# Ten small embedding tables loaded eight rows to a partition, one comparison in eight on ScalarE, and another order of units at both ends of a recommendation tower

## The reference

```
e = jnp.stack([tbl_0[ids[:, 0]], ..., tbl_25[ids[:, 25]]], axis=1)     # 2048 x 26 x 128
combined = jnp.concatenate([e, r_dense_x[:, None, :]], axis=1)
interact = jnp.einsum('bfd,bgd->bfg', combined, combined)
z = interact[:, triu_i, triu_j]                                        # 351 pairs
h = jnp.concatenate([z, r_dense_x], axis=1)
h = jnp.maximum(h @ W_top1 + b_top1, 0.0)                              # 479 -> 512
h = jnp.maximum(h @ W_top2 + b_top2, 0.0)                              # 512 -> 256
y = h @ W_top3
```

## Time and profile before

| what | value |
|---|---|
| median of 3 runs | 373.95 us (373.89 to 375.94) |
| the profiled execution | 373.27 us, of which the span is 371.4 us |
| mean granted TensorE clock | 0.986 |
| TensorE matmuls busy | 335.2 us (90%) |
| GpSimd busy | 257.3 us (69%) |
| VectorE busy | 238.5 us (64%) |
| ScalarE busy | 121.9 us (33%) |

### The profile page before, as it was taken

One profiled execution on the slowest core, in us unless ns is written; L12 is line 12 of the kernel. 1 busy time (PEld: TensorE's weight loads), 2 busy tenths in 40 slices (PEclk: granted clock), 3 DMA queues, 4 the chain that ended last, 5 costly groups with the idle time before them and its releaser, 6 DMA issues.

```text
span 371.4 us, 9558 instructions
## 1 busy us (share of the span) xinstructions
PE 335.2 (90%) x4024; PEld 310.7 (84%) x4024; DVE 238.5 (64%) x385; ACT 121.9 (33%) x229; POOL 257.3 (69%) x271
## 2 busy tenths in 40 slices
PE   0656879999999999999999999999999999967896
PEld 0646879788898999899889999899889989857795
DVE  6995499599485966679276957689277946010010
ACT  2473221332233323342233323242333224241422
POOL 5877787777777777777777777777777777775000
PEclk9998898999999999999999999999999999999999
DMA  7976228344244443434243433434243413334020
GB/s 188 287 202 196 77 73 259 91 114 101 58 120 102 123 98 98 121 104 113 58 121 100 126 91 107 112 109 113 59 136 89 117 51 108 83 108 116 19 69 4
DMA packets 40351, 41.02 MB, mean 110 GB/s; under 512 B 17119, under 2 KB 33983, under 8 KB 40308
## 3 DMA queue, kind: packets, MB, share of 16 engines
q1 hardware_dynamic: 30737, 22.44, 22.2%
q0 software_dynamic: 8448, 17.32, 17.4%
q10 hardware_dynamic: 1123, 0.64, 0.7%
HBM read 33.01 MB, written 7.36 MB: 109 GB/s over the span
## 4 chain that ended last, share of the span: by engine, by line
PE 79%; POOL 6%; DMA 4%; DVE 3%; issue 3%; ACT 3%; SPq 1%; ACTq 0%
PE ps_o L616 36%; PE ps_g L643 15%; PE ps_l L667 10%; PE ps_l L693 7%; PE ps_t L628 6%; POOL rows L257 6%; PE ps_l L669 3%; ACT h L404 2%; DMA turn<-gram 2%; DMA rows<-tbl,idx 2%; DVE onehot L525 1%; DVE tab L515 1%; PE ps_l L713 1%; DMA idx<-ids_g 1%; ACT emb L382 1%
## 5 line engine op out<-in xcount | busy, mean ns | idle before, releaser
L257 POOL DMA_INDIRECT rows<-tbl,idx x264 | 256.4, 971 | 82.9 <-issue 79.0
L525 DVE TENSOR_SCALAR onehot<-ids_b,row_of 128x513 fp32r<-128x513 int16 (+1 forms) x304 | 201.5, 740 | 18.3 <-PE ps_o L616 16.2
L616 PE MATMUL ps_o<-onehot,tab 128*128 128x256 f32 (+1 forms) x1216 | 163.4, 292 | 19.2 <-DVE tab L515 13.7
L616 PEld LDWEIGHTS ps_o<-onehot,tab 128*128 128x128 f32 (+1 forms) x1216 | 153.0, 194 | 24.7 <-issue 20.1
L539 DVE COPY gram<-ps_g 128x432 f32<-128x432 f32 x32 | 19.5, 608 | 93.1 <-PE ps_g L643 81.4
L375 ACT COPY emb<-ps_o 128x512 f32<-128x512 f32 x38 | 30.3, 797 | 129.1 <-PE ps_o L616 129.1
L643 PEld LDWEIGHTS ps_g<-emb 128*54 128x54 f32 x2048 | 54.7, 132 | 10.8 <-ACT emb L382 4.7
L643 PE MATMUL ps_g<-emb 128*54 128x54 f32 x2048 | 58.4, 216 | 5.2 <-ACT emb L382 3.5
L382 ACT COPY emb<-ps_t 128x512 f32<-128x512 f32 x66 | 43.0, 674 | 1.0 <-PE ps_t L628 0.7
L628 PE MATMUL ps_t<-ident,rows 128*128 128x128 f32 x264 | 39.0, 276 | 3.9 <-DMA rows<-tbl,idx 3.2
L667 PE MATMUL ps_l<-z,w_sb 117*128 117x256 f32 x168 | 40.9, 379 | 1.7 <-issue 1.7
(11 more groups left out here) (27 smaller groups left out, 50.0 us busy)
## 6 DMA issues: line engine op xcount, KB each, us to landing
turn<-gram SPq DMA_DIRECT2D x62, 91.1 KB
ids_b<-ids_oh SPq DMA_DIRECT2D x35, 129.0 KB, 3.6
rows<-tbl,idx POOLq DMA_INDIRECT x264
z<-turn SPq DMA_DIRECT2D x64, 40.5 KB
stage<-tbl SPq DMA_DIRECT2D x10, 256.0 KB, 5.3
stage<-tbl SPq DMA_DIRECT2D x10, 192.0 KB
turn<-gram SPq DMA_DIRECT2D x62, 21.1 KB
xs<-x SPq DMA_DIRECT2D x8, 128.0 KB, 2.2
```

The lines of the kernel that those rows point to most:

```text
L257: nc.gpsimd.indirect_dma_start(out=rows[m % RING][:, i, :], out_offset=None, in_=gathered[GATHERED.index(f)] if f in GATHERED else oh_tabl ...
L525: nc.vector.tensor_scalar(onehot[n % BUFS][0:r, 0:FILL].rearrange("p (a b) -> p a b", a=RUNS), ids_b[0:r, o, :, 0:RUN], row_of[0:r, h:h + ...
L616: last = nc.tensor.matmul(ps_o[n % 2][:, j, :], tab[0:r, UNIT * o + j, part, k, :], onehot[m % BUFS][0:r, STEP * j:STEP * (j + 1)], start= ...
```

## The change

A table is now one chunk: row 8p+k is in partition p, 125 partitions of 4 KB each, loaded by two DMAs (112 and 13 partitions), cast by one instruction and subtracted by one. The stages are 6 of 4 KB instead of 11 of 2 KB a partition. The comparison of fill h matches the rows 8p+h.

In steps 0 and 1 ScalarE makes the last fill of each unit (8 of them) in two instructions: the distance |index - row|, then max(0, 1 - distance). VectorE leaves these out.

At the start TensorE does unit (1,0) ahead of quad (0,4) and products(0), and every further unit of step 1 one place earlier. VectorE makes the comparisons of unit (1,0), the low parts of tables 6 and 7 and four comparisons more ahead of `keep_gram(0)`. In the loop TensorE does `unit(t + 1, 4)` ahead of `layer3(t - 1)`. At t = 6 it does `products(13)`, `unit(7, 4)`, `layer3(5)`, where it did `layer3(5)`, `unit(7, 4)`, `products(13)`; ScalarE and VectorE keep in that order. SyncE loads indices in another order at the start; its loop is as it was.

```diff
-KT = -(-OH_ROWS // P)
+KT = 8
+OH_P = OH_ROWS // KT
+ACT_STEPS = 2
+PIECES = ((0, OH_P // 16 * 16), (OH_P // 16 * 16, OH_P))
...
+def act_makes(t, h):
+    return t < ACT_STEPS and h == FILLS - 1
...
-        NSTAGE = 11
-        with nc.sbuf_tensor("stage", [P, NSTAGE, 512], F32) as stage:
+        NSTAGE = 6
+        with nc.sbuf_tensor("stage", [P, NSTAGE, KT * D], F32) as stage:
...
+        def made_by_act(t, o):
+            return min(unit_at(t, o) + 1, unit_at(ACT_STEPS, 0))
+        def made_by_dve(t, o, h):
+            return fill_at(t, o, h) + 1 - made_by_act(t, o) + (act_makes(t, FILLS - 1) and h < FILLS - 1)
...
             def load_ids(t, o):
                 if t and o < units_of(t - 1):
-                    sp.wait_ge(onehot_made, fill_at(t - 1, o, FILLS - 1) + 1)
+                    sp.wait_ge(onehot_made, made_by_dve(t - 1, o, FILLS - 1))
+                    if act_makes(t - 1, FILLS - 1):
+                        sp.wait_ge(onehot_act, made_by_act(t - 1, o))
...
+            def load_chunk(n):
+                if n >= NSTAGE:
+                    sp.wait_ge(chunk_l, n - NSTAGE + 1)
+                rows_of = oh_tables[n].rearrange("(p k) d -> p (k d)", k=KT)
+                for a, b in PIECES:
+                    sp.dma_start(stage[a:b, n % NSTAGE, :], rows_of[a:b, :]).then_inc(chunk_in[n % NSTAGE], 16)
...
-            for c in range(4, NCHUNKS):
-                load_chunk(c)
-                if c == NCHUNKS - 4:
-                    for o in range(UNITS):
+            for n in range(2, NOH):
+                load_chunk(n)
+                if n == NOH - 3:
+                    load_ids(1, 3)
+                    load_ids(1, 4)
+                    for o in range(FIRST_UNITS):
                         load_ids(1, o)
             load_x(1)
+            load_ids(2, 0)
             spread(0)
-            sp.wait_ge(chunk_l, NCHUNKS)
+            load_ids(2, 1)
+            load_ids(2, 2)
+            sp.wait_ge(chunk_l, NOH)
             fetch_z(0)
             load_weights()
-            for o in range(UNITS):
-                load_ids(2, o)
+            load_ids(2, 3)
+            load_ids(2, 4)
...
+            def make(t, o): 
+                n = fill_at(t, o, FILLS - 1)
+                act.wait_ge(ids_in[o], ids_loaded(t, o))
+                if n >= BUFS:
+                    act.wait_ge(onehot_used, n - BUFS + 1)
+                to = onehot[n % BUFS][0:OH_P, 0:FILL]
+                nc.scalar.activation(to.rearrange("p (a b) -> p a b", a=RUNS), ids_b[0:OH_P, o, :, 0:RUN], ACT.Abs, bias=last_row[0:OH_P]
+                                     ).then_inc(distance_made, 1)
+                act.wait_ge(distance_made, made_by_act(t, o))
+                nc.scalar.activation(to, f32(to), ACT.Relu, bias=1.0, scale=-1.0).then_inc(onehot_act, 1)
...
+            act.wait_ge(row_made, 2)
+            make(0, 0)
+            chunk(0)
+            chunk(1)
             keep_x(0)
+            chunk(2)
+            chunk(3)
+            make(0, 1)
             keep_unit(0, 0)
             keep_quad(0, 0)
+            chunk(4)
+            make(0, 2)
+            chunk(5)
             keep_unit(0, 1)
             keep_quad(0, 1)
+            chunk(6)
+            make(1, 0)
             keep_unit(0, 2)
             keep_quad(0, 2)
             keep_quad(0, 3)
+            chunk(7)
+            make(1, 1)
+            keep_unit(1, 0)
             keep_quad(0, 4)
             keep_gram(0)
...
@@ vector @@
-            makes(0, 0, FILLS)
+            makes(0, 0, 4)
+            chunk(0)
+            makes(0, 4, FILLS)
+            chunk(1)
+            for n in range(2, UNIT * FIRST_UNITS):
+                makes(0, FILLS // 2 * n, FILLS // 2 * (n + 1))
+                chunk(n)
             makes(1, 0, FILLS)
+            chunk(6)
+            chunk(7)
+            makes(1, FILLS, FILLS + 4)
             keep_gram(0)
+            makes(1, FILLS + 4, 3 * FILLS)
+            chunk(8)
+            chunk(9)
+            makes(1, 3 * FILLS, ALL)
             keep_gram(1)
             makes(2, 0, BUFS)
...
-                keep_y(t - 1)
-                keep_gram(b)
-                makes(t + 2, FILLS, BUFS)
+                if t < STEPS - 2:
+                    keep_y(t - 1)
+                    keep_gram(b)
+                    makes(t + 2, FILLS, BUFS)
+                else:
+                    keep_gram(b)
+                    keep_y(t - 1)
...
@@ tensor @@
             quad(0, 3)
+            unit(1, 0)
             quad(0, 4)
             products(0)
-            unit(1, 0)
+            unit(1, 1)
             quad(1, 0)
...
                 quad(b, 3)
-                layer3(t - 1)
-                unit(t + 1, 4)
-                products(b)
+                if t < STEPS - 2:
+                    unit(t + 1, 4)
+                    layer3(t - 1)
+                    products(b)
+                else:
+                    products(b)
+                    unit(t + 1, 4)
+                    layer3(t - 1)
```

More of the change, by code:

```diff
@@ L159, in tower_kernel, with chunk_count, parts_of @@
         f32 = lambda ap: ap.bitcast(F32)
[L162 to L189, removed]
+        def chunk_count(n):
+            return 16 * len(PIECES) * (n // NSTAGE + 1)
+        def parts_of(n):
+            return stage[0:OH_P, n % NSTAGE, :], [tab[0:OH_P, n, part].rearrange("p k d -> p (k d)") for part in range(2)]
         def unit_at(t, o):
@@ L364, in _, with chunk @@
         def _(act):
-            def chunk(c):
-                act.wait_ge(chunk_in[c % NSTAGE], chunk_count(c))
-                for _, at, hi, _ in chunk_parts(c):
-                    last = nc.scalar.copy(hi, at)
-                last.then_inc(chunk_h, 1)
+            def chunk(n):
+                act.wait_ge(chunk_in[n % NSTAGE], chunk_count(n))
+                at, (hi, _) = parts_of(n)
+                nc.scalar.copy(hi, at).then_inc(chunk_h, 1)
+            def make(t, o):
[8 more added lines that the diff above has]
+                nc.scalar.activation(to, f32(to), ACT.Relu, bias=1.0, scale=-1.0).then_inc(onehot_act, 1)
             def keep_unit(t, o):
@@ L606, in unit @@
                 if t < 2:
-                    pe.wait_ge(chunk_l, 2 * UNIT * (o + 1))
+                    pe.wait_ge(chunk_l, UNIT * (o + 1))
                 for h in range(FILLS):
                     m = fill_at(t, o, h)
-                    pe.wait_ge(onehot_made, m + 1)
-                    for i in range(KB):
-                        k = KB * h + i
-                        r = chunk_rows(k)
-                        for j in range(UNIT):
-                            for part in range(2):
-                                last = nc.tensor.matmul(
-                                    ps_o[n % 2][:, j, :], tab[0:r, UNIT * o + j, part, k, :],
-                                    onehot[m % BUFS][0:r, STEP * j:STEP * (j + 1)], start=(k, j, part) == (0, 0, 0),
-                                    stop=(k, j, part) == (KT - 1, UNIT - 1, 1), skip_group_check=True)
+                    if act_makes(t, h):
+                        pe.wait_ge(onehot_act, made_by_act(t, o))
+                    else:
+                        pe.wait_ge(onehot_made, made_by_dve(t, o, h))
+                    for j in range(UNIT):
+                        for part in range(2):
+                            last = nc.tensor.matmul(
+                                ps_o[n % 2][:, j, :], tab[0:OH_P, UNIT * o + j, part, h, :],
+                                onehot[m % BUFS][0:OH_P, STEP * j:STEP * (j + 1)], start=(h, j, part) == (0, 0, 0),
+                                stop=(h, j, part) == (KT - 1, UNIT - 1, 1), skip_group_check=True)
                     last.then_inc(onehot_used, 1)
```

90 lines of the change are left out of this document (36 added, 54 removed).

## The result

The changed kernel takes 364.5 us (median of 4 runs, 363.89 to 365.45), the kernel before, run beside it, 374.88: ratio 0.9725, 95% interval 0.9683 to 0.9767. It is faster, by more than I forecast (367.5, range 365.8 to 372.9). The profiled execution took 364.55 us with a span of 362.7, against 373.27 and 371.4: 8.7 us less in both.

The account below looks back on a forecast made before the run. TensorE's path (5.5 + 2.5 - 1.5 = 6.5 us earlier) and GpSimd's stream of indirect DMAs (6.4) were taken to bound the kernel; 373.27 - 6.4 = 366.9, median 367.5 us, range 365.8 to 372.9.

Parts of the forecast that it names:

- TensorE's path: TensorE up to layer1(6): start 5.5, loop 2.5 and tail -1.5 make it 6.5 us earlier.
- Floor of GpSimd: End of kernel: indirect DMA 264 still starts at 339.96, so products(15) gain at most 4.3 to 7.0 us; 6.4 taken.
- Loop: Waits for ScalarE ahead of `layer3`: with a unit between, five of six go, 2.5 us (between 0 and 3).
- VectorE to the end of step 1: Start: products(0) copied at 42.5, 24 comparisons and two low parts left, done at 60.8; unit (1,4) ends at 61.4.
- But GpSimd: Start: quad (1,4) arrives only at 62.7 to 65.5, so TensorE waits; lead 4.4 to 7.2, taken as 5.5 us.
- The 0.3 for the clock: Start: taken off the 5.8 us lead for a fall of the clock while TensorE waits for quad (1,4).
- Rival C: ScalarE's Abs needs another function table, two loads of 1.28 us per comparison: 375.1 us; chance 0.06 with smaller mishaps.
- Tail: At t = 6 spread(13) waits behind the store of y(5), so layer1(6) loses 1.5 us.
- A: Start: the lead is not kept, VectorE's waits eat what it saved; 1.0 us gained, 372.9 us; chance 0.15.
- B: GpSimd's stream: large table packets stall it in four waves of loads, 11.4 us later, 378.9 us; chance 0.07.
- The band from 366.4 to 369.9: Whole kernel: the forecast's time in us with floor and lead at either end; chance 0.72.

Follow-up runs that it names:

- loop_old_2: Changed kernel with the loop's order undone, `layer3(t - 1)` again ahead of `unit(t + 1, 4)`; 367.64 us, ratio 0.9862 to the kernel before.
- tail_old_2: Changed kernel with the order at t = 6 undone on TensorE, ScalarE and VectorE; 363.5 us, ratio 0.9757 to the kernel before.
- start_old: Changed kernel with unit (1,0) behind products(0) on TensorE and ScalarE, as before; 367.59 us, ratio 0.9861 to the kernel before.
- act_none: Changed kernel with all comparisons on VectorE, none on ScalarE; 371.57 us, ratio 0.9914 to the kernel before.
- tail_old: Changed kernel with the order at t = 6 undone, in a slower session; 508.89 us, ratio 0.9953 to the kernel before.
- three_gathers_2: Changed kernel without each quad's fourth indirect DMA and its lookups, in a slower session; 432.16 us, ratio 0.8430 to the kernel before.

## Why the prediction was wrong

The mechanisms were there, and their sizes weren't. The forecast was the smaller of two sums, TensorE's path (6.5 us) and the floor of GpSimd (6.4 us); both were too small, against 8.7 measured. On the path the start and the loop were short by 1.3 and 1.2 us.

**"Floor of GpSimd" was mis-sized.** The prediction took the last indirect DMA's start, 339.96, for a time that the change can't move, and so let products(15) come no earlier than 344.5. They came at 342.79. The last DMA started at 338.48, and in the other kernels' traces at 337.70 (loop_old_2), 337.62 (tail_old_2), 337.06 (start_old) and 335.93 (act_none): its long pieces fall elsewhere and are of other lengths in each kernel. Where it bit, in tail_old_2, products(15) started at 341.70, 4.08 us after the last DMA's start. By this distance the floor of the changed kernel lay at 342.56, right under the 342.79 of TensorE's path. The 6.9 us that I named as its likelier end were 8.9. I had the two long rows and used them for a rival on the slow side alone; the same rows bound a gain of up to 5.8 us, 2.85 and 2.98.

**"Loop", 2.5 us, measured 3.7.** The term was read from the row of TensorE's waits, 0.5 us each. The distance between products of tiles 2 and 3 was 17.77 us before (116.48 - 98.71) and is 17.01 now: 0.76 a step, and loop_old_2 gives back 3.7. The overlap that a wait ends, 0.25 us each time, was left out. My upper end for this term was 3.0.

**"VectorE to the end of step 1" and "But GpSimd", 5.5 us, measured 6.8.** Unit (1,1) was forecast at 43.0 and started at 42.82, which is partly luck: products(0) began at 37.90 instead of 39.4, and took 4.99 us, in part at the half clock, instead of 3.60. Nor had the prediction the 2.23 us that VectorE stood for the indices of unit (1,0), up to 28.66; it still had products(0) copied at 42.6 (forecast 42.5) and step 1 made at 60.6 (60.8). Quad (1,4) was turned at 63.27, inside the 62.7 to 65.5 of the forecast, 0.9 us ahead of the middle that I took, from a DMA that started at 58.76 instead of 59.71. The 0.3 for the clock didn't come, products(1) took 3.60, and from quad to products passed 1.37 us instead of 1.53. That makes the 1.3. That quad (1,4) was late there is shown: without its fourth DMA the wait is gone. ScalarE's comparisons took 727 and 635 ns, 1.36 us where 1.3 was assumed, and cost no second table load: one ACT_TABLE_LOAD stands in the whole trace. Rival C is out. The Trainium skill ("ScalarE: Activation LUTs", section "Table sets: the hidden batching unit") has relu, copy and abs in every set, and the trace agrees.

**"Tail", -1.5 us, measured -1.9, by the right chain.** Spread(13) starts 9.63 us after products(13), forecast 9.6, right behind the stores of y. Layer1(6) follows at 20.0, forecast 19.5 (9.6 and the 9.94 from 328.01 to 337.95). The half microsecond lies in SyncE's queue: the spread landed sooner, with fetch_z(13) starting 5.34 us after it instead of 5.86, but the seven DMAs of fetch_z(13) took 3.34 us to go out instead of 2.54, and layer1(6) came 1.70 after them instead of 1.54. Why these DMAs took longer is open. The landing is no constant: in loop_old_2, start_old and act_none fetch_z(13) starts 6.55 to 7.1 us after the spread, and the tail is 20.7 to 21.0. That the term came out within 0.4 us is in part luck.

Right beside this chain stands a second one, and it is the one that the profile's own chain follows. TensorE stood 2.14 us for quad (14,3), then made products(14) at the half clock, until 329.07, and layer1(6) started 0.23 us later. Of what layer1(6) waits for, only z of tile 13 was still to come. So the rows and the clock hold this place almost as long as SyncE does, which no row of before announced. The window 324 to 328 of the changed kernel (length, busy, PEclk, DMA share, GB/s):

```profile
324.00:328.00 4.00, 4.00 (x92) 0.50 0.40 103
```

**The rivals.** A, no lead at the start, is refuted by the 6.8 us at products(1). Undoing the unit's place costs 2.2 us there, undoing ScalarE's part 3.7; against the kernels of their own session they are some 3.2 and 4.7. That the two are independent no run shows, and the layout of the tables was not tried by itself, so the rest of the 6.8 can't be given. B, GpSimd held up by larger packets, did not come: there are more long indirect DMAs, but shorter ones, and the stream ends earlier. For the gathers themselves, the last indirect DMA of quad (0,4) landed 6.34 us after its start (30.05 to 36.39) and 6.30 in start_old, where before it took 5.76: 0.6 us slower, and earlier all the same, because it started 1.5 us earlier. The Trainium skill ("DMA: Bandwidth & Descriptors", section "Queues, rings and completion order") has each engine drain a whole packet of one queue, some 9 to 17 descriptors, before it turns to the next queue. The 0.6 us points the way that the prediction took from this rule; that the larger packets are its cause isn't shown.

**The sum.** 6.8 + 3.7 - 1.9 = 8.6, against 5.5 + 2.5 - 1.5 = 6.5. Without the floor the forecast would have moved by 0.1 us, from 6.4 to 6.5. Nor would the range have held the time: TensorE's path with each term at its upper end gives 7.2 + 3.0 - 1.5 = 8.7 us, that is 364.6 for the profiled execution and, with the 0.7 that the prediction adds for the median, 365.3. The measured median of 364.5 lies under that too, since it stood 0.05 us below the profiled execution and not 0.7 above it. The band from 366.4 to 369.9 doesn't come out of the prediction's own ends either: 373.95 less 4.3 and 7.0 is 369.7 and 367.0.

## What to carry to other kernels

A wait that the profile gave as 0.5 us cost TensorE 0.75 here: measure what it is worth as the distance between the same stage of two steps. Before a difference of a microsecond is given a cause, look how far kernels with the same code up to that point are apart: here 1.2 us at products(1). A stream that runs on its own is no fixed floor where it holds long pieces without a releaser; give it both signs. When work is reordered on one engine, follow each result into the queue that it passes next: here a store of 1 KB stood ahead of the eight DMAs that the tail hung on.

## What was not expected of the hardware

The same kernels take 504 to 518 us in some sessions and 363 to 374 in others (with all their gathers). The slower sessions were on three chips, the two faster ones on two others, so chip and session can't be told apart. tail_old and tail_old_2 are one kernel: 508.89 us with a mean granted clock of 0.865, and 363.5 with 0.986. In the slower session TensorE's time goes in gaps ahead of the small products, which have no releaser in the profile; the wait table of tail_old:

```profile
PE ps_g L664 <- issue: 78.0, 89, 5.1
```

In tail_old_2 these matmuls have no such row; they are also busy 59.4 us there and 97.2 in tail_old. With a quarter less indirect DMAs the kernel falls to 432 us and the gaps of this kind to 31.9 us (three_gathers_2). That points at GpSimd's DMAs or their queue, without showing it; what the gaps are was not tried. GpSimd's own long indirect DMAs, of 1.2 to 3.9 us where 0.95 is usual, come in every fifth place at the start of the changed kernel (numbers 7, 12 and 17), then as 23 and 34. In the traces of the faster sessions none comes after the first 55 us; tail_old, of a slower one, has one of 2.49 us at 89.56. Their cause is open as well.
